# Values as the stationary operand in a decoder's first attention, with two transpose banks

## The chip, the core and the metric

The kernel runs on one core of a Trainium2 chip. A core has five engines that run their own instruction lists side by side and wait for each other through semaphores: TensorE (PE in the profile, with its weight loads as PEld), VectorE (DVE), ScalarE (ACT), GpSimd (POOL) and SyncE (SP), which here only issues DMA transfers. The metric is the device time of one execution in microseconds, the median of the runs.

## The reference

Two decoder layers over x, 16 sequences of 64 tokens with 128 features, all in fp32. Each layer has three parts with a layer norm ahead of each: a self-mixing part, a cross-attention over 64 context tokens of 96 features, and a mixture of 8 experts. The change touches only the first part of the first layer:

```python
qkv = jnp.einsum('bse,ef->bsf', inputs, qkv_kernel) + qkv_bias
qkv_heads = qkv.reshape(b, heads, s, -1)          # 16 heads, 64 rows, 3 x 8
q, k, v = jnp.split(qkv_heads, 3, axis=-1)
qk = jnp.einsum('bhse,bhte->bhst', q, k) * scale
attn = jax.nn.softmax(qk + causal_mask, axis=-1)
out = jnp.einsum('bhst,bhte->bhse', attn, v).reshape(b, s, e)
x = x + out
...
```

The reshape of (s, 384) to (heads, s, 24) cuts the token axis: one head of a sequence consists of 4 tokens, each of which gives 16 rows of 24 numbers. So a head has 64 rows and 8 features, and the head's output has to be put back into 4 tokens of 128 features.

## The kernel before, in words

The program is written by hand for each engine, in one list of calls per engine (`transpose_probs(3)`, `weigh_values(2)`, ...). The lists were ordered by a planner, and their order is the order of work on that engine; semaphores set only who waits for whom. PSUM has eight banks of 128 x 512 fp32 (`bank[0]` to `bank[7]`).

*Into the attention.* The projected q, k and v are stored to a scratch array in memory and loaded back with heads in place of features (SP, lines 389 and 394). A few spreading operations make block forms of them: KB and QA, and for the values Vb, a view of the tile `att`, which is filled with zeros first (line 449) and given a column of ones per head (line 487).

*The attention* works on 16 units u of eight heads each, two units being one pair m of sequences. On TensorE:
- `scores(m)` (lines 749 and 758) writes the causal mask and the scores of units 2m and 2m+1 to two of the banks 0 to 3.
- VectorE then does `row_max(u)` (line 1843) and `subtract_max(u)` (line 1850) into one of three buffers Es, and ScalarE `exponentials(u)` (line 1413) in place.
- `transpose_probs(u)` (line 776) transposes the four 128 x 128 blocks of Es to bank 4, and ScalarE's `copy_probs(u)` (line 1419) copies them to one of two buffers PTs. The next transposes wait for that copy.
- `weigh_values(u)` (line 792) has eight products. The transposed probabilities are the stationary operand (128 x 64); the values, 8 features and a one for two heads, are the moving operand (18 columns). Outputs go to bank 5 or 6, with 64 query rows on each half of the partitions; the ninth column is the sum of the probabilities.
- VectorE's `inverse(u)` and `normalise(u)` (lines 1829 and 1835) divide by these sums, into a tile with positions on the partitions.

An fp32 product is two records of matmul and two of weight load in the trace.

*Out of the attention*, per half of the batch h: `outputs_by_feature` (line 804) transposes, ScalarE copies (line 1427), SP stores to the scratch array `o_scratch` (line 418) and loads it back with features on the partitions (line 421), and `outputs_by_token` (line 822) transposes to tokens, which VectorE's `add_attention` (line 1856) adds to X. The layer norm of the cross-attention follows. Once all scores are out, SP also issues the weights of the last expert block (lines 425 and 427), whose place in Wb is then free.

*Behind it* stand the cross-attention (with the keys and values of the second layer, `keys_values1`, as filler), the first experts (`up0_first`, `up0_third`, `down0`, lines 884, 897 and 916), the state-space part of the second layer (`inject`, `widen`, lines 928 and 936; `add_states` on VectorE), the second cross-attention (`scores1`, `weigh_values1`, lines 976 and 999) and the last experts with a search for the routing threshold (`count`, line 1068).

## Time and profile before

| | |
|---|---|
| Runs | 257.46 us median (256.94 to 261.43, three runs) |
| Span of the profiled execution | 255.3 us (its own time beside this span was not recorded) |
| TensorE busy | 239.0 us, 94% |
| VectorE busy | 175.9 us, 69% |
| ScalarE busy | 141.8 us, 56% |
| GpSimd busy | 77.9 us, 31% |
| Granted TensorE clock | full speed in every stretch that was asked for |

The span runs from the first to the last instruction of one execution. A busy share is a mean over stages with different limits; which engine sets the time of a stage is read from the chain of waits, which follows the work back from the last instruction to what released it.

### The profile page before, as it was taken

How to read it: one execution, taken by the hardware profiler on the slowest of the kernel's cores; microseconds unless marked ns; L12 is line 12 of the kernel's file. 1: busy time of each engine (PE TensorE's matmuls, PEld its weight loads, DVE VectorE, ACT ScalarE, POOL GpSimd, SP SyncE). 2: the span in 40 equal slices, each digit the busy share in tenths (PEclk: the TensorE clock that was granted, in tenths of full speed). 3: DMA queues.
4: the chain of work that ended last, by engine and by line, in shares of the span. 5: the costliest groups of instructions: out<-in, count | busy, mean ns of one | idle time of the engine just before them, and what ended most of it. 6: DMA issues, size and time to landing. Idle time of an engine off the chain costs nothing.

```text
span 255.3 us, 5508 instructions
## 1 busy us (share of the span) xinstructions
PE 239.0 (94%) x1993; PEld 163.9 (64%) x1994; DVE 175.9 (69%) x602; ACT 141.8 (56%) x293; POOL 77.9 (31%) x137
## 2 busy tenths in 40 slices
PE   8988899998999999999999886999998999999995
PEld 8555577774535766756593534678887566577775
DVE  5465699874878836445217979957655688889975
ACT  0764776764264688467657445465565744544540
POOL 7856900001040474667465051533401000000000
DMA  5888960178100000000000000000000000000002
GB/s 136 173 196 245 302 152 0 31 220 205 44 1 0 1 3 0 0 1 3 0 1 3 1 0 0 3 3 3 3 5 0 3 0 0 1 3 0 0 3 82
DMA packets 24040, 11.64 MB, mean 46 GB/s; under 512 B 13017, under 2 KB 23006, under 8 KB 24014
## 3 DMA queue, kind: packets, MB, share of 16 engines
q1 hardware_dynamic: 22973, 10.94, 16.5%
q0 software_dynamic: 80, 0.20, 0.7%
q8 instruction: 16, 0.26, 0.4%
q10 hardware_dynamic: 960, 0.16, 0.3%
q14 instruction: 11, 0.08, 0.1%
HBM read 8.68 MB, written 2.62 MB: 44 GB/s over the span
## 4 chain that ended last, share of the span: by engine, by line
PE 73%; DVE 15%; ACT 5%; issue 3%; POOL 2%; DMA 1%; DVEq 0%; POOLq 0%; ACTq 0%
PE bank L1029 10%; PE bank L1041 10%; PE bank L897 6%; PE bank L884 6%; PE bank L916 6%; PE bank L776 3%; DVE stats L1720 3%; PE bank L1014 3%; PE bank L758 2%; PE bank L976 2%; PE bank L648 2%; PE bank L792 2%; PE bank L693 2%; PE bank L986 2%; PE bank L999 2%
## 5 line engine op out<-in xcount | busy, mean ns | idle before, releaser
L516 POOL TENSOR_TENSOR X<-X,att 128x128 f32<-128x128 f32 x72 | 30.4, 457 | 29.2 <-ACT att L1469 29.1
L441 POOL TENSOR_TENSOR rs<-rs,halves 128x4 f32<-128x4 f32 x14 | 14.9, 1063 | 61.8 <-DVE rs L1735 61.1
L1029 PE MATMUL bank<-XT,Wb 128*128 128x512 f32 x64 | 29.9, 599 | 0.0
L1041 PE MATMUL bank<-Wb,att 128*128 128x128 f32 x224 | 27.2, 278 | 0.0
L1041 PEld LDWEIGHTS bank<-Wb,att 128*128 128x128 f32 x224 | 26.1, 192 | 1.4 <-issue 1.4
L1905 DVE SCALAR_TENSOR_TENSOR att<-bank,cols,att 128x512 f32<-128x512 f32 x18 | 13.5, 749 | 16.8 <-ACT att L1458 7.8
L1469 ACT ACTIVATE att<-bank,comb 128x128 f32<-128x128 f32 x72 | 20.2, 383 | 6.9 <-PE bank L916 6.8
L1509 ACT ACTIVATE att<-bank 128x512 f32<-128x512 f32 x32 | 18.7, 599 | 9.7 <-PE bank L1029 9.7
L916 PEld LDWEIGHTS bank<-W2a,att 128*128 128x128 f32 x144 | 18.0, 192 | 5.0 <-issue 3.6
L916 PE MATMUL bank<-W2a,att 128*128 128x128 f32 x144 | 18.7, 276 | 0.0
L884 PE MATMUL bank<-XT,W1a 128*128 128x512 f32 x36 | 18.2, 595 | 0.0
L897 PE MATMUL bank<-XT,W3a 128*128 128x512 f32 x36 | 18.1, 598 | 0.0
L1517 ACT ACTIVATE big<-bank 128x512 f32<-128x512 f32 x14 | 8.3, 596 | 17.1 <-PE bank L1041 17.1
L1458 ACT ACTIVATE att<-bank,cols 128x512 f32<-128x512 f32 x18 | 12.6, 699 | 9.5 <-DVE att L1905 7.1
L1029 PEld LDWEIGHTS bank<-XT,Wb 128*128 128x128 f32 x64 | 11.2, 192 | 9.4 <-issue 8.8
L2042 DVE SCALAR_TENSOR_TENSOR X<-big,rt,X 128x128 f32<-128x128 f32 x56 | 15.4, 347 | 2.6 <-ACT big L1517 2.4
L1742 DVE TENSOR_SCALAR XN<-X,mv,rs 128x128 f32<-128x128 f32 x48 | 14.1, 356 | 4.1 <-POOL rs L441 3.8
L1720 DVE BATCH_NORM_STATS2 stats<-X 128x6 f32<-128x128 f32 x48 | 10.4, 280 | 7.1 <-POOL X L516 5.3
L1419 ACT ACTIVATE PTs<-bank 128x512 f32<-128x512 f32 x16 | 9.5, 595 | 8.0 <-PE bank L776 5.8
L529 POOL TENSOR_TENSOR Es<-Es,sm 128x512 f32<-128x512 f32 x8 | 8.2, 1044 | 14.2 <-DVE sm L1965 14.2
L1843 DVE TENSOR_REDUCE mx<-bank 128x8 f32<-128x512 f32 x16 | 10.5, 678 | 2.4 <-PE bank L758 2.4
L776 PE MATMUL bank<-ident,Es 128*128 128x128 f32 x64 | 10.2, 283 | 1.9 <-ACT PTs L1419 1.6
(229 smaller groups left out, 484.1 us busy)
## 6 DMA issues: line engine op xcount, KB each, us to landing
Wb<-in_L_ffn_W SPq DMA_DIRECT2D x1, 1024.0 KB, 5.5
Wb<-in_L_ffn_W SPq DMA_DIRECT2D x8, 128.0 KB, 5.2
X<-in_x SPq DMA_DIRECT2D x2, 256.0 KB, 3.1
k_scratch<-QKVT SPq DMA_DIRECT2D x1, 512.0 KB, 3.9
q_scratch<-QKVT SPq DMA_DIRECT2D x1, 512.0 KB, 4.7
Wb<-k_scratch SPq DMA_DIRECT2D x1, 512.0 KB, 4.6
v_scratch<-QKVT SPq DMA_DIRECT2D x1, 512.0 KB, 6.1
V<-q_scratch SPq DMA_DIRECT2D x1, 512.0 KB, 6.2
```

The lines of the kernel that those rows point to most:

```text
L441: nc.gpsimd.tensor_tensor(rs[:, 0, cut], rs[:, 1, cut], halves[:, :], ALU.pow).then_inc(l_root[h], 1)
L516: nc.gpsimd.tensor_tensor(X[:, h * HT + t, :], X[:, h * HT + t, :], part0[:, i % 2, t, :], ALU.add).then_inc(f_acc, 1)
L776: last = nc.tensor.transpose(bank[4][:, p4 * P:(p4 + 1) * P], Es[:, u % 3, p4 * P:(p4 + 1) * P], ident[:, :])
L884: mm(bank[i % 2][:, :], W1a[:, e, :], XT[:, half(h)], start=True, stop=True).then_inc(f_h1, 1)
L897: mm(bank[2 + i % 2][:, :], W3a[:, e, :], XT[:, half(h)], start=True, stop=True).then_inc(f_h3, 1)
L916: last = mm(bank[4 + i % 2][:, t * P:(t + 1) * P], hid0[:, i % 2, t * P:(t + 1) * P], W2a[:, e, :], start=not shared, stop=True, skip_grou ...
L1029: mm(bank[i % 4][:, :], W1b[:, e, f * P:(f + 1) * P], XT[:, half(h)], start=True, stop=True).then_inc(m_up, 1)
L1041: last = mm(bank[4 + h][:, t * P:(t + 1) * P], hid[:, e % 2, f, tile], W2b[:, e, f, :], start=(f == 0), stop=(f == F1 - 1))
L1469: AF(part0[:, i % 2, t, :], bank[4 + i % 2][:, t * P:(t + 1) * P], ACT.Copy, scale=comb[:, tt, e:e + 1]).then_inc(f_part, 1)
L1509: AF(hid[:, e % 2, f, half(h)], bank[i % 4][:, :], ACT.Gelu).then_inc(m_gelu, 1)
L1720: last = V.bn_stats(stats[:, t, :], src[:, t, :])
L2042: last = V.scalar_tensor_tensor(X[:, t, :], ys[:, e, t, :], rt[:, 9, t, e:e + 1], X[:, t, :], ALU.mult, ALU.add)
```

## The change

Five things are done in the first attention.

1. `weigh_values` works on pairs m. The values of one head are the stationary operand (128 x 32: two blocks of 16 columns, the first nine of which are used, the sum's column among them), and the transposed probabilities stream as 64 columns. Sixteen products per pair go in turn to the four groups of 32 output partitions of bank 6.
2. `transpose_probs` writes to banks 4 and 5 in turn, so it waits for the copy of the unit before the last.
3. The division leaves the units. ScalarE's `values_out(m)` copies the undivided outputs and sums from bank 6. `inverse`, `normalise` and `outputs_by_feature` go.
4. The scratch array has whole rows (128 x 1024 per half), stored in one transfer and loaded in four: two for the outputs, two for the sums, in pieces of 256 bytes.
5. The sums are transposed to tokens (`sums_by_token`), inverted (`sums_inverse`), and `add_attention` multiplies the token outputs by them before it adds.

The zero fill of `att` now covers the whole tile and stands later in GpSimd's list. All lists were written out anew, in the last expert block too, where a loop stood before.

```diff
-    VW = HD + 1
+    VW = 16
...
-        Opos = att[:, VP:VP + N].rearrange("p (h q e b u) -> p h q e b u", h=2, q=NP4, e=HD, b=HB)
-        OT2 = big[:, 12 * N:12 * N + HALF].rearrange("p (c x) -> p c x", c=CH)
+        OV = [big[:, first:first + N].rearrange("p (c y t m) -> p m y c t", c=CH, m=HT, t=GT) for first in (12 * N, 15 * N)]
+        OVrows = [big[:, first:first + N] for first in (12 * N, 15 * N)]
...
-                sp.wait_ge(o_act[h], 1)
-                sp.dma_start(o_d[h, :, :].rearrange("(c e) (b u x) -> e b u c x", e=HD, b=HB, u=2)
-                             .rearrange("e b u c x -> (e b u) c x"), OT2).then_inc(st_o[h], 16)
+                sp.wait_ge(a_out, HT * (h + 1))
+                sp.dma_start(o_d[h, :, :], OVrows[h]).then_inc(st_o[h], 16)
                 sp.wait_ge(st_o[h], 16)
-                sp.dma_start(OT[:, half(h)], o_d[h, :, :]).then_inc(ld_o[h], 16)
+                blocks = o_d[h, :, :].rearrange("(j n v) (c x) -> n v c j x", j=NP4, n=2, c=CH)
+                for n in range(2):
+                    sp.dma_start(OT[:, half(h)].rearrange("p (n j x) -> p n j x", n=2, j=NP4)[:, n, :, :],
+                                 blocks[n, 0:HD, :, :, :].rearrange("e c j x -> (e c) j x")).then_inc(ld_o[h], 16)
+                for n in range(2):
+                    sp.dma_start(SU[:, half(h)].rearrange("c (n j x) -> c n j x", n=2, j=NP4)[:, n, :, :],
+                                 blocks[n, HD, :, :, :]).then_inc(ld_s[h], 16)
...
-            nc.gpsimd.memset(att[:, 0:VP], 0.0).then_inc(c_fill, 1)
...
+            nc.gpsimd.memset(att[:, :], 0.0).then_inc(c_fill, 1)
+            pool.wait_ge(c_fill, 4)
...
             def transpose_probs(u):
                 pe.wait_ge(a_exp, u + 1)
-                if u >= 1:
-                    pe.wait_ge(a_trc, u)
-                else:
+                if u >= 2:
+                    pe.wait_ge(a_trc, u - 1)
+                if u == 0:
                     pe.wait_ge(v_copied, 1)
+                if u == 1:
+                    pe.wait_ge(pow_ready, 1 + len(POWER_OF))
                 for p4 in range(NP4):
-                    last = nc.tensor.transpose(bank[4][:, p4 * P:(p4 + 1) * P],
+                    last = nc.tensor.transpose(bank[4 + u % 2][:, p4 * P:(p4 + 1) * P],
                                                Es[:, u % 3, p4 * P:(p4 + 1) * P], ident[:, :])
...
+            def weigh_values(m):
+                pe.wait_ge(a_trc, 2 * m + 2)
+                if m == 0:
                     pe.wait_ge(vb_act, 2)
...
+                if m >= 1:
+                    pe.wait_ge(a_out, m)
+                for i in range(NP4):
+                    for j in range(NP4):
+                        head = NP4 * j + i
+                        u2, first = head // HD, (head % HD) * S
+                        last = mm(bank[6][j * 2 * VW:(j + 1) * 2 * VW, i * S:(i + 1) * S],
+                                  Vb[:, m, head, :, :].rearrange("p n v -> p (n v)"),
+                                  PTs[:, u2, first:first + S], start=True, stop=True)
...
+            def sums_by_token(h):
+                pe.wait_ge(ld_s[h], 32)
...
+                for t in range(HT):
+                    last = nc.tensor.transpose(bank[7 - 2 * h][:, t * CH:(t + 1) * CH],
+                                               SU[:, half(h)].rearrange("c (x m) -> c m x", m=HT)[:, t, :], ident[0:CH, 0:CH])
...
             def outputs_by_token(h):
-                pe.wait_ge(ld_o[h], 16)
+                pe.wait_ge(ld_o[h], 32)
                 if h == 0:
-                    pe.wait_ge(o_act[0], 1)
+                    pe.wait_ge(o_inv[0], 1)
...
             def copy_probs(n):
                 act.wait_ge(a_tr, n + 1)
                 if n >= 2:
-                    act.wait_ge(a_pv, n - 1)
-                AF(PTs[:, n % 2, :], bank[4][:, :], ACT.Copy).then_inc(a_trc, 1)
+                    act.wait_ge(a_pv, n // 2)
+                AF(PTs[:, n % 2, :], bank[4 + n % 2][:, :], ACT.Copy).then_inc(a_trc, 1)
...
+            def values_out(m):
+                act.wait_ge(a_pv, m + 1)
+                AF(OV[m // HT][:, m % HT, :, :, :], bank[6][:, 0:2 * P].rearrange("p (y c t) -> p y c t", c=CH, t=GT), ACT.Copy
+                   ).then_inc(a_out, 1)
...
+            def sums_inverse(h):
+                dve.wait_ge(o_sums[h], 1)
+                V.reciprocal(rO[:, h, :, :], bank[7 - 2 * h][:, 0:HT * CH].rearrange("p (t c) -> p t c", c=CH)
+                             ).then_inc(o_inv[h], 1)
...
             def add_attention(h):
                 dve.wait_ge(x_psum[h], 1)
-                then(V.tensor_tensor(X[:, tiles(h), :], bank[7 - h][:, :].rearrange("p (t d) -> p t d", d=D),
-                                     X[:, tiles(h), :], ALU.add))
+                dve.wait_ge(o_inv[h], 1)
+                then(V.tensor_tensor(XN[:, tiles(h), :].rearrange("p t (c e) -> p t c e", e=HD),
+                                     bank[7 - h][:, :].rearrange("p (t e c) -> p t c e", e=HD, c=CH),
+                                     rO[:, h, :, :].unsqueeze(3).broadcast_to([P, HT, CH, HD]), ALU.mult))
+                then(V.tensor_tensor(X[:, tiles(h), :], XN[:, tiles(h), :], X[:, tiles(h), :], ALU.add))
```

How the order moves, at three places. TensorE, the last units of the attention, before (L776 are transposes of probabilities, L792 the value products, L822 the first half's outputs by token, L767 filler, L804 the second half's outputs by feature):

```order
L792 MATMUL bank<-att,PTs 64x18 x8
L776 MATMUL bank<-ident,Es 128x128 x4
L792 MATMUL bank<-att,PTs 64x18 x8
L822 MATMUL bank<-ident,OT 128x128 x4
L776 MATMUL bank<-ident,Es 128x128 x4
L792 MATMUL bank<-att,PTs 64x18 x8
L776 MATMUL bank<-ident,Es 128x128 x4
L792 MATMUL bank<-att,PTs 64x18 x16
L767 MATMUL bank<-causal,perm 128x512 x2
L804 MATMUL bank<-ident,att 128x128 x4
```

The same place now (L784 transposes, L755 and L764 scores, L800 value products, L812 sums, L830 outputs by token, L675 filler):

```order
L784 MATMUL bank<-ident,Es 128x128 x8
L755 MATMUL bank<-causal,perm 128x512 x2
L764 MATMUL bank<-big,Wb 128x4x64 x4
L800 MATMUL bank<-PTs,att 32x64 x16
L784 MATMUL bank<-ident,Es 128x128 x8
L800 MATMUL bank<-PTs,att 32x64 x16
L812 MATMUL bank<-ident,big 128x16 x4
L830 MATMUL bank<-ident,OT 128x128 x4
L784 MATMUL bank<-ident,Es 128x128 x8
L800 MATMUL bank<-PTs,att 32x64 x16
L675 MATMUL bank<-maskf,Wk 128x512
```

Two units of transposes stand together, and one group of value products follows a pair; ahead of the last two groups no scores are left. After the last group comes other work at once, no transpose of outputs.

ScalarE in the same stretch, before (L1413 exponentials, L1419 copies of transposed probabilities, L1427 outputs by feature):

```order
L1413 ACTIVATE Es<-Es 128x512 x2
L1419 ACTIVATE PTs<-bank 128x512 x2
L1427 ACTIVATE big<-bank 128x4x16x4 x2
L1413 ACTIVATE Es<-Es 128x512 x2
L1419 ACTIVATE PTs<-bank 128x512
L1413 ACTIVATE Es<-Es 128x512
L1419 ACTIVATE PTs<-bank 128x512 x2
```

and now (L1452 exponentials, L1458 copies of transposed probabilities, L1462 `values_out`):

```order
L1452 ACTIVATE Es<-Es 128x512 x2
L1458 ACTIVATE PTs<-bank 128x512 x2
L1462 ACTIVATE big<-bank 128x4x16x4
L1452 ACTIVATE Es<-Es 128x512 x2
L1462 ACTIVATE big<-bank 128x4x16x4
L1458 ACTIVATE PTs<-bank 128x512 x2
```

Each pair has one more copy, which stands in line with the exponentials and the copies of the next pair.

TensorE at the end of the first experts, before (L916 and L912 are down-projections and their bias, L936 `widen`):

```order
L916 MATMUL bank<-W2a,att 128x128 x4
L936 MATMUL bank<-ST,Apow 128x2x60
L936 MATMUL bank<-ST,Apow 128x2x56
L936 MATMUL bank<-ST,Apow 128x2x52
L912 MATMUL bank<-b2a,OT 128x128 x4
L916 MATMUL bank<-W2a,att 128x128 x4
L936 MATMUL bank<-ST,Apow 128x2x48
```

and now (L924, L920 and L944):

```order
L924 MATMUL bank<-W2a,att 128x128 x4
L920 MATMUL bank<-b2a,OT 128x128 x4
L924 MATMUL bank<-W2a,att 128x128 x4
L944 MATMUL bank<-ST,Apow 128x2x60
L944 MATMUL bank<-ST,Apow 128x2x56
L944 MATMUL bank<-ST,Apow 128x2x52
L944 MATMUL bank<-ST,Apow 128x2x48
```

The group `widen(0, 1)` of three matmuls has moved from before the last down-projection to behind it.

## Rows read from the trace of the kernel before

**Rows 1.** The page, busy us with share of span and instruction count.

```profile
PE 239.0 (94%) x1993; PEld 163.9 (64%) x1994; DVE 175.9 (69%) x602; ACT 141.8 (56%) x293; POOL 77.9 (31%) x137
```

**Rows 2.** Busy time by stage: stretch, length, then PE, PEld, DVE, ACT, POOL, clock, DMA.

```profile
26.50:59.30 32.80, 30.23 (x414) 23.31 (x416) 27.85 (x75) 21.43 (x39) 6.14 (x5) 1.00 0.56 146
59.30:80.80 21.50, 20.52 (x113) 10.78 (x113) 14.72 (x56) 10.60 (x19) 2.59 (x2) 1.00 0.21 47
80.80:134.70 53.90, 53.90 (x295) 35.97 (x294) 26.45 (x77) 35.87 (x98) 31.45 (x72) 1.00 0.00 1
134.70:161.30 26.60, 21.54 (x164) 11.34 (x162) 23.54 (x90) 13.05 (x24) 8.59 (x10) 1.00 0.01 2
```

**Rows 3.** Chain of waits in the attention: start us, us, what.

```profile
35.27 0.61 ACT PTs L1419
...
36.02 0.63 PE bank L776 x4
36.64 0.32 PE bank L749 x2
36.97 0.86 PE bank L758 x8
...
48.42 1.04 PE bank L792 x32
...
58.61 0.66 PE bank L792 x16
```

**Rows 4.** Chain of waits in later stages.

```profile
94.18 0.86 PE bank L897 x2
...
126.76 0.36 PE bank L928 x8
...
129.06 0.66 PE bank L936 x6
...
165.13 0.62 PE bank L999 x32
```

**Rows 5.** VectorE by line, 26 to 62 us: form, count, busy us, mean ns, idle before.

```profile
L1850 DVE TENSOR_TENSOR Es<-bank,mx 128x512 f32<-128x512 f32 x16 | 10.6, 679 | 0.6 <-PE bank L776 0.4
L1843 DVE TENSOR_REDUCE mx<-bank 128x8 f32<-128x512 f32 x16 | 10.5, 678 | 2.4 <-PE bank L758 2.4
L1835 DVE TENSOR_TENSOR att<-bank,rO 128x64 f32<-128x64 f32 x16 | 3.7, 259 | 0.2
L1829 DVE RECIPROCAL rO<-bank 128x8 f32<-128x8 f32 x16 | 3.0, 194 | 2.5 <-PE bank L792 2.5
```

**Rows 6.** ScalarE by line, 20 to 62 us.

```profile
L1413 ACT ACTIVATE Es<-Es 128x512 f32<-128x512 f32 x16 | 9.6, 627 | 2.4 <-DVE Es L1850 2.2
L1419 ACT ACTIVATE PTs<-bank 128x512 f32<-128x512 f32 x16 | 9.5, 595 | 8.0 <-PE bank L776 5.8 <-PE bank L792 2.1
L1427 ACT ACTIVATE big<-bank 128x256 f32<-128x256 f32 x4 | 1.3, 383 | 2.3 <-PE bank L804 2.3
```

**Rows 7.** Timeline, SP's issues and the transposes behind them: start us, us, instruction.

```profile
53.06 5.13 SPq L427 DMA_DIRECT2D Wb<-in_L_ffn_W  x8
...
61.23 0.37 SPq L418 DMA_DIRECT2D o_scratch<-big  x1
...
64.19 0.34 SPq L421 DMA_DIRECT2D OT<-o_scratch  x1
...
66.94 0.53 PEld L822 LDWEIGHTS bank<-ident,OT 128*128 128x128 f32 x4 [0.51 <-DMA OT<-o_scratch]
```

**Rows 8.** Transfers: issues, KB each, median us from issue to landing.

```profile
v_scratch<-QKVT SPq DMA_DIRECT2D x1, 512.0 KB, 6.1
...
o_scratch<-big SPq DMA_DIRECT2D x2, 256.0 KB, 3.0
```

**Rows 9.** Timeline of GpSimd: the fill of att, and its wait for the keys.

```profile
1.65 2.02 POOL L449 MEMSET att<- 128x2304 f32 x1
...
21.04 6.81 POOL L494 TENSOR_SCALAR big<-Wb,pairs 128x512 f32<-128x512 f32 x4 [4.20 <-DMA Wb<-k_scratch]
```

More of the change, by code:

```diff
@@ L533, in _ @@
             root(2, 0)
+            root(2, 1)
             add_part(0, 0, 0)
@@ L808, in power @@
+                last.then_inc(o_sums[h], 1)
             def power(r):
@@ L1069, in count @@
                    start=True, stop=True).then_inc(r_cnt, 1)
-            def count_next(rounds):
-                i = next(rounds, None)
-                if i is not None:
-                    count(i)
-                if i == SEARCH:
-                    prefix()
             def prefix():
@@ L1308, in _ @@
             up1(0, 1, 1)
[L1310 to L1320 removed]
+            up1(1, 0, 0)
+            count(0)
+            up1(1, 1, 0)
+            up1(1, 0, 1)
+            count(1)
+            down1(0, 1)
+            count(2)
+            up1(1, 1, 1)
+            up1(2, 0, 0)
+            count(3)
+            up1(2, 1, 0)
+            up1(2, 0, 1)
+            count(4)
+            down1(1, 0)
+            count(5)
+            down1(1, 1)
+            count(6)
+            up1(2, 1, 1)
+            up1(3, 0, 0)
+            count(7)
+            up1(3, 1, 0)
+            up1(3, 0, 1)
+            count(8)
+            down1(2, 0)
+            count(9)
+            down1(2, 1)
+            count(10)
+            up1(3, 1, 1)
+            up1(4, 0, 0)
+            up1(4, 1, 0)
+            count(11)
+            up1(4, 0, 1)
+            up1(4, 1, 1)
+            up1(5, 0, 0)
+            count(12)
+            down1(3, 0)
+            count(13)
+            down1(3, 1)
+            count(14)
+            up1(5, 1, 0)
+            up1(5, 0, 1)
+            up1(5, 1, 1)
+            count(15)
+            prefix()
+            down1(4, 0)
+            down1(4, 1)
+            down1(5, 0)
+            down1(5, 1)
+            up1(6, 0, 0)
+            up1(6, 1, 0)
+            up1(6, 0, 1)
+            down1(6, 0)
+            up1(6, 1, 1)
+            up1(7, 0, 0)
+            up1(7, 1, 0)
+            up1(7, 0, 1)
+            up1(7, 1, 1)
+            down1(6, 1)
             down1_last()
@@ L2232, in _ @@
             route()
-            for e in range(E1 - 1):
-                add_expert(e)
+            add_expert(0)
+            add_expert(1)
+            add_expert(2)
+            add_expert(3)
+            add_expert(4)
+            add_expert(5)
+            add_expert(6)
             add_last()
```

471 lines of the change are left out of this document (211 added, 260 removed).

## Prediction

> **What bounds the kernel now.** I read five views. The page's busy shares come first [rows 1]: TensorE 94% of the span, everything else far below; that is an average. The busy time by stage is second [rows 2]; I cut the span where the work changes. The reader is to see that the first attention (26.5 to 59.3 us) has TensorE busy for 30.2 of 32.8 us and VectorE for 27.9; that the feed-forward behind it (80.8 to 134.7) has TensorE busy throughout; and that from 134.7 to 161.3 VectorE leads. So a gain in the attention survives if TensorE reaches the feed-forward earlier: what follows there is a fixed amount of TensorE work.
>
> The chain of waits inside the attention is third [rows 3]. It runs mostly on TensorE, but it also goes through ScalarE's copy of the transposed probabilities: copy, then the next transpose, since all transposes use bank 4. Two batches of weigh_values take 1.04 us together; the last begins at 58.61 and ends at 59.27 (its 0.66 added).
>
> The same chain in other stages shows what small matmuls cost [rows 4]; the lists by line give VectorE's and ScalarE's instructions [rows 5, 6]; the timeline of the transfers gives the way of the second half's outputs through memory [rows 7].
>
> **The change: value matmuls.** Before, 16 batches of 8 products (16 records each, since an fp32 product is two records): 32 records in 1.04 us [rows 3], so 8.3 us in all. Now there are 8 groups of 16 products, also 32 records each, with 64 moving columns, 32 output columns and four column groups in turn. No row has this shape with 64 columns. Bounds, per group: below, weigh_values1, 32 records of 64 moving columns over four quarters of the array, 0.62 us; above, the rate of inject, four groups of 32 columns but 128 moving columns, 8 records in 0.36 us, so 32 in 1.44; and with no overlap at all 16 times an eighth of a 512-column product, 16 x 0.86/8 = 1.72 [rows 4]. I take 0.62: inject has the same four groups, and its 0.36 for four 128-column products, which one after another would be 4 x 0.86/4 = 0.86, shows that the groups overlap; weigh_values1 has the same moving length. Saved on TensorE: 8 x (1.04 - 0.62) = 3.4 us. The feature transposes go (two groups of four, 0.63 us each by the transposes of [rows 3]); two groups of four 16-row transposes of the sums come. I cost these at 0.25 us each, estimated below a full group's 0.63.
>
> **VectorE** loses 16 reciprocals and 16 multiplies, 3.0 + 3.7 = 6.7 us [rows 5]. It gains two small reciprocals and two 128x512 multiplies, which I price as the subtraction of the same size, 0.68 each, and which lie in add_attention. **ScalarE** loses four 0.38 us copies and gains eight 128x256 copies out of the bank. Nearest row: those same copies, 0.383; with elements 16 bytes apart they could cost as much as a 512-element copy, 0.595, and not less than 0.383 [rows 6]. I take 0.383.
>
> **The period.** One period is two batches of scores (0.32 + 0.86), two groups of transposes (2 x 0.63) and a value group (0.62): TensorE 3.06 us [rows 3, 4]. ScalarE: 2 x 0.627 + 2 x 0.595 + 0.383 = 2.83 [rows 6], and five hand-overs of some 0.04, so 3.03. VectorE: 2 x (0.679 + 0.678) = 2.71 [rows 5]. Three engines within 0.35 us, in fixed orders: I take 3.2. Added waits: a value group waits until ScalarE has emptied the one before (0.383), with transposes and scores in between to cover it; the copies of a pair wait for the value group of the pair before, which is in the period. The second transpose bank is what lets TensorE write one group while ScalarE still copies the other. Start: the first transposes wait for scores 1.2, two maxima 1.36 (the second maximum now stands ahead of the first subtraction), a subtraction 0.68 and an exponential 0.63: 26.5 + 3.9 = 30.4. The eighth period starts at 30.4 + 7 x 3.2 = 52.8. Sums and outputs of the first half stand ahead of it: 0.25 + 0.63 and a wait of some 0.4 for the reciprocal. Then transposes 1.26, the uncovered copy 0.6 + 0.1, the group 0.62: it ends near 56.7, not 59.27. That is **-2.6**.
>
> **The way out of the second half.** Before, from the end of the last batch (59.27) to the store (61.23) stood reciprocal, multiply, transposes and copies: 1.96 us [rows 3, 7]. Now one copy: 56.7 + 0.4 = 57.1, 4.1 earlier. But the last block's weights go through the same queue. Their last eight issues took from 53.06 to 58.19, and the store came 3.0 us after; now they follow the last scores, 30.4 + 5 x 3.2 + 1.3 + 1.2 = 48.9, end near 54.6, and the store comes 2.5 us after. It took 3.0 us, and the slowest store of a scratch array in this kernel 6.1 [rows 8]; below 3.0 I see no reason to go, since it writes twice the bytes (in 128 long rows instead of 2048 pieces). I take 4.0, nearer to its own row. The reload is four issues of some 0.4 us instead of one: outputs land one issue later, the sums two more behind them. So the outputs are transposed near 57.1 + 4.0 + 0.4 + 2.8 = 64.3; before 66.94 [rows 7]. Lead: 2.6. VectorE then has a multiply and a reciprocal more before the layer norm, 0.68 + 0.20, so **1.7** of lead arrives, and TensorE, in order, enters the feed-forward 1.7 earlier.
>
> **Behind it.** The tables were written anew for all engines. In the feed-forward TensorE has the same work. One place changes the path: the group widen(0, 1), 0.66 us [rows 4], stood ahead of the last down-projection and now stands behind it, and that projection's output starts the VectorE-bound stage: **-0.7**. add_bias moves behind two weigh_probs on POOL, which is idle for two thirds of that stage [rows 2]: nothing. The fill of att grows from 2304 to 4096 columns and moves to just before the ones in it. At 2.02 us for 2304 it takes 3.6; POOL waited 4.2 us there for keys from memory [rows 9], which cover it by 0.6. Without that cover the late halves of the keys would slip, and only scores(4), the fifth of eight, needs them. The count rounds of the last block: the first stands one up-projection earlier (0.86), but the end follows TensorE's work: nothing. At the start v is projected ahead of the context; its store can leave up to one projection earlier (0.86), but q's load, on which the first scores wait, keeps its place in SP's order: nothing.
>
> **Sum:** -2.6 + 0.9 (lead lost on the way out) - 0.7 = -2.4. The profiled execution has a span of 255.3; the median of the three runs is 257.46, 2.2 above that span. So 252.9 of span, and **255.0** of time. A measurement of this kernel tells about 2% from no change (under 252.3, over 262.6).
>
> **A rule against the change.** In [rows 6] ScalarE's copies are already 0.6 of each 1.2 us that it spends on a batch, and now it alone empties the value bank. By those rows it is 0.03 us a period below TensorE. The Trainium skill (TensorEngine Tiling (Array Packing), section Performance Considerations) says that tiling speeds up TensorE but not the emptying of PSUM, that the copies may become the limit, and that both ScalarE and VectorE should share them; by that rule ScalarE sets the period here. What it makes of the time is the second rival.
>
> **Rivals.**
> - *The four column groups do not overlap* (or at inject's rate). The decision point is a value group of 0.76 us: above it TensorE's period passes 3.2. At 1.44 the stage grows by 8 x 0.68 = 5.4: 260.4, slower than before; at 1.72, 262.7. For it: no row with 64 columns in four groups, and inject's rate if it is per record. Against: inject's own 0.36 instead of 0.86. 5%.
> - *ScalarE sets the period, nothing is won.* If the strided copy costs 0.595 and every exponential waits its turn in ScalarE's order, the period is 3.5 to 3.7, as now (8 of them fill most of the 32.8 us). Then only widen and part of the way out are left: about 257. For it: three engines nearly equal, latencies uncovered at the last two periods. Against: VectorE had 6.7 us more and that goes. 17%.
> - *The reload lands late.* Store 6.1 instead of 4.0 because the last block's weights are ahead of it in the queue, reload the same with four times the issues: outputs near 68 or 69. TensorE has some 7.7 us of work between (59.27 to 66.94 before), to about 64.4, so it waits some 4 us: 259. For it: the shorter distance to the weights. Against: the same store took 3.0. 5%.
> - *More is won.* The whole lead of 4.1 is kept, the extra VectorE work hides behind the sums, and the search's earlier start gives its 0.86: -4.1 - 0.7 - 0.9 = 251.8. 18%.
>
> The forecast itself has 55%: 252.9 to 257. The range is 251.6 to 258.2: it leaves out part of the last rival and both slow ones. Faster by over 2%: most of "more is won", 0.17. Slower by over 2%: 0.04 (the groups without overlap, or two of these at once). Within: 0.79.
>
> **What would show it.** Value groups of 32 records at about 0.6 us in the chain; the line of the copies out of the transpose banks gone from the chain between transposes; the last value group ending near 56.7; the second half's outputs transposed near 64.3; the stage from 80.8 and the one from 134.7 moved earlier by 1.7 and 2.4 us with the same lengths. It is wrong if a value group takes over 0.76, if ScalarE has no idle time in the attention, or if TensorE waits for the reload.

## The result, and the profile after

The changed kernel takes 256.33 us (median of 20 runs, 254.86 to 261.34); the kernel before, run beside it, 257.42 (20 runs, 256.94 to 261.43). The ratio is 0.9941, with a 95% interval from 0.9918 to 0.9964: a small gain, within 2%. The forecast was 255.0, with a range of 251.6 to 258.2.

The times are told here together with the mean granted TensorE clock of each run, because without it they can't be understood: of the 20 runs of the change one had a mean clock of 0.999 and took 254.86 us; eight at 0.993 took 255.18 to 256.11; seven at 0.986 or 0.987 took 255.62 to 257.48; the four at 0.98 or less took 257.88 to 261.34.

The profiled execution took 256.76 us, span 255.0, mean clock 0.986. Its page, in the form of [rows 1], and the row of the granted clock in 40 slices of the span (a digit is tenths of full speed):

```profile
PE 238.0 (93%) x1994; PEld 162.3 (64%) x1994; DVE 173.3 (68%) x574; ACT 142.3 (56%) x297; POOL 79.3 (31%) x137
PEclk9999599999999999999999999999999999999999
```

VectorE has 2.6 us less work than in [rows 1], TensorE 1.0 less. New is the 5: in the fifth slice TensorE ran at about half its clock. The windows below are read as [rows 2]: stretch, length, busy us of PE, PEld, DVE, ACT, POOL, then the clock, the share of DMA, GB/s.

```profile
23.00:24.00 1.00, 0.42 (x4) 0.28 (x2) 0.00 (x0) 0.67 (x2) 0.91 (x2) 1.00 0.58 193
25.00:26.00 1.00, 0.38 (x3) 0.09 (x2) 0.45 (x1) 0.83 (x3) 0.91 (x2) 0.91 0.91 324
26.00:27.00 1.00, 0.59 (x3) 0.56 (x5) 0.13 (x1) 0.27 (x1) 0.91 (x2) 0.50 1.14 348
...
31.00:32.00 1.00, 1.00 (x6) 0.35 (x5) 0.19 (x1) 0.95 (x2) 0.93 (x2) 0.50 1.22 304
32.00:33.00 1.00, 1.00 (x8) 1.00 (x6) 1.00 (x2) 0.16 (x1) 0.37 (x1) 0.67 0.98 298
...
26.50:59.30 32.80, 30.19 (x420) 21.87 (x421) 25.36 (x49) 23.81 (x44) 6.57 (x6) 0.91 0.60 168
```

From just before 26 to about 32.7 us the clock is at 0.50, which is 1.2 GHz of 2.4. In the microseconds before, TensorE was busy for 0.42 and 0.38 of a microsecond: the new early order has the key products done earlier, and TensorE then waits for copies of the powers and for q. The kernel before has its key products there; the same view of it shows it at full clock:

```profile
23.00:24.00 1.00, 1.00 (x5) 0.37 (x5) 0.00 (x0) 0.83 (x2) 1.00 (x1) 1.00 0.70 277
...
25.00:26.00 1.00, 0.78 (x5) 0.29 (x3) 0.59 (x1) 0.51 (x2) 1.00 (x1) 1.00 0.98 283
```

The chain of waits of the changed kernel, through the attention and out of it (start us, us, what; compare [rows 3]):

```profile
26.41 2.08 PE bank L764 x8
28.49 1.04 PE bank L740 x4
...
30.07 1.71 PE bank L764 x8
31.78 1.46 PE bank L784 x8
...
33.56 0.86 PE bank L764 x8
...
37.66 0.58 PE bank L800 x32
...
49.49 0.65 PE bank L800 x32
...
56.21 0.70 PE bank L800 x32
...
56.93 0.61 ACT big L1462
...
57.56 4.19 DMA o_scratch<-big
...
62.18 2.69 DMA OT<-o_scratch
...
64.92 0.75 PE bank L830 x4
65.66 0.59 PE bank L812 x4
66.28 0.57 DVE rO L1900
...
66.94 0.70 DVE XN L1919
67.67 0.70 DVE X L1922
```

Eight score records (the second group, at 30.07) take 1.71 us at half clock and 0.86 at full; the four transposes of the values take 1.04, and 0.66 at full clock in the profile of c3 below. Value groups take 0.58 to 0.70. The last ends at 56.91 us; before it was 59.27 [rows 3]. The second half's outputs are transposed at 64.92; before 66.94 [rows 7]. Then come two steps in line that the kernel before didn't have there: the sums' transposes and the reciprocal, and a product (L1919) ahead of the sum (L1922).

ScalarE's and VectorE's lines, in the form of [rows 5, 6]:

```profile
L1462 ACT ACTIVATE big<-bank 128x256 f32<-128x256 f32 x8 | 4.9, 617 | 0.9 <-PE bank L800 0.8
...
L1900 DVE RECIPROCAL rO<-bank 128x64 f32<-128x64 f32 x2 | 1.1, 558 | 1.3 <-PE bank L812 1.3
```

How much of the lead is left further on has to be read where the same work is done in both orders. The first up-projection is no such mark: `up0_first` came first before (77.81), and now `up0_third` stands ahead of it and of the gate (75.35). Two marks that are: the transposes of the cross-attention behind one group of `up0_first` and two of `up0_third`, and the last down-projection of the first experts. Before:

```profile
80.46 0.38 PE L844 MATMUL bank<-ident,QKVT 128*128 128x128 f32 x2
132.29 1.16 PE L916 MATMUL bank<-W2a,att 128*128 128x128 f32 x8
```

and now:

```profile
79.77 0.38 PE L852 MATMUL bank<-ident,QKVT 128*128 128x128 f32 x2
132.20 1.16 PE L924 MATMUL bank<-W2a,att 128*128 128x128 f32 x8
```

The last product ends at 252.34 us (before 252.61). So in these two profiles 2.4 us are won at the end of the attention, 0.7 are left where the feed-forward has begun, 0.1 at its last down-projection, and 0.3 at the end.

### The profile page after: what moved, and what is told of

Read it like the earlier page. It is cut to its first block, busy times and chain, and to the rows that moved or that the text cites. A ratio compares the mean times of both kernels' runs of the same rounds, so it can differ in the third digit from the quotient of the medians.

```text
span 255.0 us, 5486 instructions
## 1 busy us (share of the span) xinstructions
PE 238.0 (93%) x1994; PEld 162.3 (64%) x1994; DVE 173.3 (68%) x574; ACT 142.3 (56%) x297; POOL 79.3 (31%) x137
## 4 chain that ended last, share of the span: by engine, by line
PE 70%; DVE 15%; DMA 7%; ACT 3%; issue 2%; POOL 1%; SPq 0%; DVEq 0%
PE bank L1037 11%; PE bank L1049 10%; PE bank L924 7%; PE bank L905 6%; PE bank L892 5%; PE bank L1022 3%; PE bank L764 3%; PE bank L784 3%; DMA V<-q_scratch 3%; PE bank L640 3%; PE bank L984 2%; DVE stats L1795 2%; PE bank L800 2%; PE bank L654 2%; DMA q_scratch<-QKVT 2%
## 5 line engine op out<-in xcount | busy, mean ns | idle before, releaser
L446 POOL TENSOR_TENSOR rs<-rs,halves 128x4 f32<-128x4 f32 x14 | 14.3, 1022 | 81.3 <-DVE rs L1810 77.8
L924 PEld LDWEIGHTS bank<-W2a,att 128*128 128x128 f32 x144 | 18.3, 191 | 6.2 <-issue 4.0
L924 PE MATMUL bank<-W2a,att 128*128 128x128 f32 x144 | 19.1, 278 | 0.0
L1369 ACT ACTIVATE XT<-bank 128x512 f32<-128x512 f32 x12 | 7.1, 593 | 9.0 <-PE bank L654 9.0
L1458 ACT ACTIVATE PTs<-bank 128x512 f32<-128x512 f32 x16 | 8.8, 595 | 4.4 <-PE bank L784 4.4
```

Of the source, the lines that this page charges most:

```text
L446: nc.gpsimd.tensor_tensor(rs[:, 0, cut], rs[:, 1, cut], halves[:, :], ALU.pow).then_inc(l_root[h], 1)
L924: last = mm(bank[4 + i % 2][:, t * P:(t + 1) * P], hid0[:, i % 2, t * P:(t + 1) * P], W2a[:, e, :], start=not shared, stop=True, skip_grou ...
```

## Experiments

Line numbers move with the edits. **Where the clock went** was the first question. My theory: TensorE falls to 1.2 GHz because it idles at 23 to 26 us, and that costs what the change wins. The rivals: q's load sets the start anyway, or what is won early is lost later.

**a1_hold**: the gaps filled.

```diff
+            def hold(n):
+                for _ in range(n):
+                    mm(bank[4][:, 0:P], XT[:, 0:P], XT[:, 0:P], start=True, stop=True)
...
                 if m == 0:
+                    hold(4)
                     pe.wait_ge(kb_early, NP4)
...
+            hold(3)
             power(5)
+            hold(2)
             power(6)
```

> The changed kernel with nine plain fp32 products of 128 columns added on TensorE (three ahead of the fifth group of powers, two ahead of the sixth, four in the first scores group between its mask products and its wait for keys and queries); their results go to a bank that nobody reads. They fill the gaps of 22.95 to 26.4 us. Theory A, the clock: in the profile of the change TensorE idled there and its granted clock was 0.50 from about 26 to 32.7 us; the first eight score products took 2.08 us where the same eight took 0.86 before. With the gaps filled the granted clock is 1.00 in that stretch, the first score group takes 0.86, the first transposes start near 30.4 instead of 31.7, the last value group ends near 55.4 instead of 56.9, and the median goes from 256.3 to 254.9 (1.2 to 1.6 us less). Theory B, the start of attention is set by the load of q and by VectorE and ScalarE: the clock may come back, but the last value group ends within 0.4 of 56.9 and the median within 0.4 of 256.3. Theory C, what is won early is lost again behind the attention: the last value group ends near 55.4 and the median stays within 0.4 of 256.3.

Measured: 256.21 us median of 12, 254.66 to 260.18; ratio to the kernel before 0.9936 (0.9899 to 0.9973). Its windows:

```profile
24.00:26.00 2.00, 2.00 (x15) 1.54 (x15) 0.51 (x1) 1.71 (x4) 1.91 (x2) 1.00 0.88 305
...
156.00:158.00 2.00, 0.72 (x15) 0.50 (x17) 1.97 (x6) 0.63 (x1) 0.99 (x1) 1.00 0.00 0
...
160.00:162.00 2.00, 2.00 (x33) 1.78 (x32) 1.90 (x6) 0.72 (x2) 1.52 (x2) 0.50 0.00 0
```

The early clock is back, and the last value group starts at 54.45 us instead of 56.21, 1.8 us earlier, as theory A had it (1.5). But the median didn't follow, so its forecast of the time failed. The rows show why: in this execution the clock fell at 159 us instead, behind another stretch in which TensorE was busy for 0.72 of 2 us. (The change's own profile has 0.73 of 2 us there and keeps its clock, so such a stretch doesn't always bring a fall.) Five of the 12 runs stayed at 0.999 or 1.0, and these took 254.66 to 255.05; five at 0.987 took 256.78 to 257.92.

**a2_old_early** and **a3_new_early** exchange the early order alone, the lists of TensorE and ScalarE up to the first probabilities: a2 is the change with the list of before, a3 the reverse. The core of a2:

```diff
-            power(1)
-            keys0(0)
-            power(2)
...
+            power(4)
+            keys0(0)
+            power(5)
+            keys0(1)
+            power(6)
```

> The changed kernel with the order of the early work (first products to the first score groups, on TensorE and on ScalarE) as the kernel before has it; attention and everything behind it as changed. Theory A, the clock: TensorE again has its key products and powers at 23 to 25.3 us, the granted clock stays 1.00 from 25 to 33 us, and the median is 254.9 (1.2 to 1.6 us under the change). Theory B, the early order costs nothing, or gains: median within 0.4 of 256.3, or up to 1 us slower because the keys of the later cross attention are copied later.

Measured: 257.79 us median of 12 (257.20 to 261.12), no run above 0.993. Theory A failed here, and the median lies 0.5 above what theory B allowed.

```profile
30.00:32.00 2.00, 0.76 (x6) 0.66 (x7) 1.80 (x4) 1.75 (x4) 1.93 (x2) 1.00 1.22 298
32.00:34.00 2.00, 2.00 (x12) 1.50 (x12) 0.69 (x1) 2.00 (x4) 0.11 (x1) 0.58 0.98 281
```

With the old early order the clock holds to 32 us and falls then, behind a stretch in which TensorE was busy for 0.76 of 2 us while it waited for the first probabilities. So the early order alone isn't the cause: with the other order the gap lies elsewhere, and the fall came behind it.

> The kernel before with only the early order of the change, on TensorE and on ScalarE. Theory A, the clock: the granted clock falls to 0.50 at 26 to 32 us here too, the first score groups and transposes take twice as long, and the median is 1.0 to 1.8 us above the kernel before (258.4 to 259.2). Theory B, the early order is harmless: within 0.4 of 257.4.

Measured: 258.55 us median of 12 (256.79 to 261.71), ratio 1.0022 (0.9985 to 1.0059). Three runs at 1.0 took 256.79 to 257.34, as the kernel before does at 1.0 (256.94 to 257.55). So at full clock the early order itself costs nothing. Whether it makes more runs lose the clock isn't shown: 9 of 12 did, against 17 of 29 of the kernel before beside them (49 of 79 in all comparisons). The median lies where theory A had it, but the interval takes in no change as well as a loss of 1.5 us. The profiled execution has the same gap as the change, and kept its clock:

```profile
25.00:26.00 1.00, 0.36 (x3) 0.06 (x2) 0.46 (x1) 0.82 (x3) 0.91 (x2) 1.00 0.99 324
26.00:27.00 1.00, 0.60 (x6) 0.63 (x8) 0.11 (x1) 0.26 (x1) 0.91 (x2) 1.00 1.09 344
```

**b4_hold_both** also fills TensorE's gaps in the second cross attention.

```diff
+                    if t == 0:
+                        hold1(3)
                     pe.wait_ge(c_qc[t // HT], 4)
...
+            hold1(6)
             scores1(2)
             transpose_xn(4, 1, 6)
             scores1(3)
+            hold1(2)
             queries1(1, 0)
```

> The changed kernel with the nine filling products of the first experiment, and eleven more of 128 columns in the gaps of TensorE at 152 to 161 us (three before the second cross attention's first scores wait for their queries, six before its third score group, two behind its fourth). Their results are read by nobody. In the runs of the change the time follows the granted clock: 254.86 us at a mean of 0.999, 255.2 to 256.1 at 0.993, 256.5 to 257.5 at 0.987; with the first filling alone the five runs at 0.999 or 1.0 took 254.66 to 255.05 and the six at 0.992 to 0.987 255.6 to 257.9, and the profile of one of these had its 0.50 at 159 to 166 us. Theory A, the clock falls where TensorE idles: with both gaps filled nearly all runs are at 0.999 or more, and the median is 254.7 (1.6 under the change). Theory B, the falls at 159 us come whatever TensorE does: the runs split as with the first filling, and the median is 256.0 to 256.3.

Measured: 255.91 us median of 12 (255.13 to 259.21), ratio 0.9909 (0.9877 to 0.9942). Six of 12 runs at 0.999 or 1.0, where theory A had nearly all. In the profiled execution the clock fell at a third place, near 52 us, where TensorE waits ahead of the last value groups. The products themselves cost: the runs at 0.999 or 1.0 take 255.13 to 255.75, with the first nine products alone (a1) 254.66 to 255.05.

**c3_hold_lite** keeps seven of those eleven (three and four).

> The changed kernel with the nine early filling products and seven later ones (three and four; the four others of the kernel with both fillings are left out, since behind the read-out of the second half that kernel's profile took 104.57 us to the last product and the change's 104.08). Theory A: the runs stay at a mean clock of 0.999 or more as with all eleven, and the half microsecond comes back: median 254.8. Theory B: with fewer products the clock falls again in half of the runs: median 255.5 to 256.

Measured: 255.23 us median of 6 (254.68 to 255.73), ratio 0.9917 (0.9901 to 0.9933); five of the six at 1.0. In these runs the clock mostly stays, and the half microsecond came back in part (255.09 by the middle run at 1.0, b4 255.34).

**d1_before_hold** puts such products into the kernel before.

```diff
                 if m == 0:
+                    hold(4)
                     pe.wait_ge(kb_early, NP4)
...
+                    if t == 0:
+                        hold1(3)
                     pe.wait_ge(c_qc[t // HT], 4)
...
+            hold1(4)
             scores1(2)
```

> The kernel before, its own order and its own attention, with eleven filling products of 128 columns on TensorE (four ahead of the first scores' wait for keys and queries, three and four in the second cross attention's gaps at 152 to 160 us). Theory A, the granted clock falls where TensorE has idled: runs of the kernel before at a mean of 1.0 took 257.0 to 257.5 (18 of 51), and the filled one shows 1.0 in most runs and a median of 257.1. Then the change at an undisturbed clock is worth 257.1 against 254.7 to 255.3, 1.8 to 2.4 us, twice what its plain median shows. Theory B, the falls in the kernel before come from elsewhere: the runs split as before, median 257.5 to 258.4.

Measured: 257.47 us median of 12 (257.37 to 259.72), ratio 1.0006 (0.9976 to 1.0036). Nine of 12 runs at 1.0, where 30 of 79 runs of the kernel before are at 0.999 or more, but 8 of the 17 beside it. That points to TensorE's idling in this kernel too; 12 runs don't show it. It isn't faster, since the products cost the kernel before 0.3 to 0.4 us at full clock.

In all, the seven kernels with both gaps filled (b4, c3, b8, b7, b2h, c1, e1) had 40 of 52 runs at 0.999 or more; the change 1 of 20. The change was not run again beside them, so this compares different series of runs; the kernel before, which stood beside the seven, had 18 of 50.

**What the parts are worth.** **a4_one_bank** takes the second transpose bank away.

```diff
-                if u >= 2:
-                    pe.wait_ge(a_trc, u - 1)
+                if u >= 1:
+                    pe.wait_ge(a_trc, u)
...
-                    last = nc.tensor.transpose(bank[4 + u % 2][:, p4 * P:(p4 + 1) * P],
+                    last = nc.tensor.transpose(bank[4][:, p4 * P:(p4 + 1) * P],
```

> The changed kernel with one bank for the transposed weights instead of two: each transpose waits for the copy of the one before. If the period of the attention is set by TensorE's work (3.06 us of it in 3.2), the wait for each copy, 0.6 us of ScalarE for every four transposes, puts about 0.5 us into each of eight periods that other matmuls cover in part: the last value group ends 1 to 3 us later and the median is 1 to 3 us above the change. If other work always stands between two transposes, as in the kernel before, nothing: within 0.4 of 256.3.

Measured: 264.48 us median of 6 (261.52 to 266.46), ratio 1.0171 (1.0122 to 1.022). Its two runs at 1.0 took 261.52 and 261.76 us, 6.8 over the change at 0.999. The timeline of TensorE:

```profile
41.29 0.65 PE L800 MATMUL bank<-PTs,att 128*32 128x64 f32 x32
45.22 0.66 PE L800 MATMUL bank<-PTs,att 128*32 128x64 f32 x32
```

The period is 3.9 us instead of 3.0: in every one of the eight periods TensorE stands for 0.7 to 0.8 us between the two groups of transposes, waiting for the copy. (The clock of this execution fell only at 58 us.) The size was over twice what I expected; with one bank, in this order of work, the change would be slower than the kernel before.

**b8_no_division** (base: b4, both fillings) leaves out the division of the second half.

```diff
             outputs_by_token(1)
-            sums_by_token(1)
...
-            sums_inverse(1)
...
+                if h == 1:
+                    cut = X[:, tiles(h), :].rearrange("p t (c e) -> p t c e", e=HD)
+                    then(V.tensor_tensor(cut, bank[7 - h][:, :].rearrange("p (t e c) -> p t c e", e=HD, c=CH), cut, ALU.add))
+                    return
```

> The kernel with both fillings, and without the division of the second half's outputs: its sums are loaded but not transposed nor inverted, and the transposed outputs are added to the residual as they are, in one VectorE step. This leaves a part of the computation out. Theory A, the three steps in line (0.59, 0.57 and 0.70 in the profile of the change) are what ate the lead: 1.9 us less than with both fillings alone, or 1.4 to 1.9. Prediction's price for them was 0.25, 0.20 and 0.68, of which 0.88 on the path: 0.9 to 1.1 less. Theory B, something behind them sets the entry to the feed-forward stage: less than 0.3.

Measured: 254.11 us median of 6 (253.86 to 254.99), ratio 0.9848 (0.9797 to 0.99). At 0.999 or 1.0 it takes 253.86 to 254.13, both fillings alone 255.13 to 255.75: 1.2 to 1.4 less (254.09 against 255.34 by the middle runs at 1.0, 254.03 against 255.46 with those at 0.999). In the two profiles the way from the second half's transposes to the first `up0_first` takes 11.8 us, with the division 13.1: what is saved there arrives at the end. That lies between theory A and the prediction's price.

**b7_sums_hold** (same base) has the sums ahead of the outputs; on SP's queue too, the two loads into SU stand ahead of the two into OT.

```diff
+            sums_by_token(1)
             outputs_by_token(1)
-            sums_by_token(1)
```

> The kernel with both fillings, and the sums' loads ahead of the outputs' loads on SP's queue, and for the second half the sums' transposes ahead of the outputs' on TensorE (as the first half has them). In the profile of the change the second half's transposes at 64.92 are followed by the sums' transposes (0.59), the reciprocal (0.57), the product (0.70) and the sum (0.70); before, the sum alone followed. Theory A, these steps in line are what ate the lead of 2.0 us between 64.9 and 77: with the sums ahead, transposes and reciprocal lie beside the load of the outputs (2.69), which comes up to 0.9 later because it is queued second: the product begins 0.3 to 1.1 earlier and the median is 0.3 to 1.1 under that with both fillings alone. Theory B, the lead is lost to the order on TensorE ahead of the gate (transposes, queries and an up-projection in line from 73.6 to 77.1): no change, within 0.25.

Measured: 255.35 us median of 6 (255.23 to 257.06), as both fillings alone at full clock (255.34): no gain, as theory B had it. The timeline:

```profile
63.06 0.65 PE L817 MATMUL bank<-ident,big 16*128 16x16 f32 x4
63.64 0.75 PE L835 MATMUL bank<-ident,OT 128*128 128x128 f32 x4
...
64.02 0.42 DVE L1951 TENSOR_TENSOR QKVT<-QKVT,sm 128x256 f32<-128x256 f32 x1
64.36 0.55 DVE L1915 RECIPROCAL rO<-bank 128x64 f32<-128x64 f32 x1
65.02 0.69 DVE L1934 TENSOR_TENSOR XN<-bank,rO 128x512 f32<-128x512 f32 x1
```

The sums were there at 63.7, but the reciprocal waited in VectorE's list behind the cross attention's probabilities until 64.36, and the outputs came later, behind them. The product starts at 65.02; in c3's chain, with the sums behind, at 65.18.

**b2h_widen_back** (same base) puts widen(0, 1) back.

```diff
             down0(1, 7)
+            widen(0, 1)
             down0(1, 8)
-            widen(0, 1)
```

> The kernel with both fillings, and one widening step of the states (three products of 128 by 128 with 0.66 us a group, ahead of the read-out) put back ahead of the last down-projection, where the kernel before has it. The prediction took 0.7 us for its move behind that projection. Theory A, the move is worth that: 0.5 to 0.8 us slower than both fillings alone. Theory B, the step only waits for another engine's copy of the states at either place: within 0.25. Theory C, the move was a loss, since the read-out of the first half came 0.8 later in the change: 0.4 to 0.8 faster.

Measured: 255.50 us median of 11 (255.37 to 256.61), ten at 1.0; both fillings alone 255.34 at 1.0, b7 255.32. From the gate to the last product it took 176.0 us, b7 175.8. The move is worth about 0.2, not 0.7: theory B. The profiles show why: with the step behind the projection, the next step (`widen(0, 2)`) waits 0.38 us for VectorE's copy of the states, which the projection covers where the step stands ahead of it.

**c1_gate_early** (base: c3) moves the gate, on TensorE first, then on VectorE.

```diff
             cross0_q(1)
-            up0_third(0, 0)
-            cross0_scores(1)
             gate(0)
+            cross0_scores(1)
+            up0_third(0, 0)
...
+            gate0(0, 0)
             gate_first(0)
+            gate0(0, 1)
             gate_second(0)
-            gate0(0, 0)
```

> That kernel (nine and seven filling products) with the first half's gate moved ahead of the last cross-attention scores and of the first up-projection on TensorE, its softmax ahead of those scores' on VectorE and ScalarE, and the first two products of the feed-forward on VectorE ahead of the choice of experts; the gate's transposes go behind the second down-projection. Theory A, the gate's chain on VectorE (78.2 to 83.1 in the profile of the change) sets when the feed-forward gets going: 1.0 to 1.6 us less than without the move. Theory B, TensorE has work of its own from 66 us on (its gaps between 75 and 84 sum to under 0.5 us in the profile with the sums first): 0 to 0.4 less.

Measured: 254.93 us median of 5 (254.55 to 255.78), ratio 0.9906 (0.9889 to 0.9924): 0.3 under c3 (0.2 by the middle runs at 1.0), theory B. In its profile the clock fell near 52 us again:

```profile
51.00:52.00 1.00, 0.35 (x3) 0.25 (x3) 0.56 (x1) 0.59 (x2) 0.00 (x0) 1.00 1.07 340
52.00:53.00 1.00, 0.91 (x5) 0.94 (x6) 0.00 (x0) 0.00 (x0) 0.00 (x0) 0.57 1.08 369
```

The profile of c3 has the same 0.35 in that microsecond, and 1.00 of clock in the next.

**e1_way_out** (base: c1) shortens the way out: the nine loads of expert weights leave the loop over the halves and follow it, the first half's sums go to bank 1 instead of 7, and its outputs' transposes move up.

```diff
                 sp.dma_start(o_d[h, :, :], OVrows[h]).then_inc(st_o[h], 16)
...
-                if h == 0:
-                    sp.wait_ge(a_scores, NU)
...
+            sp.wait_ge(a_scores, NU)
...
+            outputs_by_token(0)
             weigh_values(6)
             sums_by_token(0)
-            outputs_by_token(0)
             transpose_probs(14)
```

> The kernel with the gate moved ahead, and four changes on the way out of the attention: the loads of the second layer's expert weights (nine, 5.7 us of issues on SP's queue, until 55.0 us) go behind both halves' stores and reloads; the first half's sums go to another bank, so that its outputs' transposes don't wait for the reciprocal (0.74 us in which TensorE stood, with the last probabilities' transposes queued behind); those outputs' transposes go into the wait ahead of the seventh value group; and the last probabilities' transposes follow the sums at once. Theory A, the end of the attention is set by what stands ahead of its last transposes on TensorE and the store then by SP's queue and by the transfers beside it: the last value group, at 54.4 us in the kernel with both fillings, starts near 53.1, the second half's outputs are transposed at 61.0 to 61.5 instead of 63.2, and the median is 1.0 to 1.7 us under that with the gate moved (253.2 to 253.9). Theory B, VectorE's list from 61 to 72 us or the first half's own chain sets the entry to the feed-forward: outputs earlier, but the median within 0.4 of 254.9.

Measured: 254.21 us median of 6 (253.98 to 254.84), ratio 0.9871 (0.9844 to 0.9898), all six at 1.0: the best version here, 0.7 under c1, between the theories.

```profile
53.38 0.65 PE L806 MATMUL bank<-PTs,att 128*32 128x64 f32 x32 [0.74 <-ACT PTs L1472]
...
61.41 1.03 PE L779 MATMUL bank<-causal,perm 128*128 128x512 bf16 x4 [0.16 <-issue]
62.27 0.63 PE L835 MATMUL bank<-ident,OT 128*128 128x128 f32 x4
...
54.73 0.34 SPq L418 DMA_DIRECT2D o_scratch<-big  x1
57.38 0.93 SPq L422 DMA_DIRECT2D OT<-o_scratch  x2
```

The store takes 2.65 us, from its issue to that of the loads, instead of 4.38 (c3's chain) now that the weights aren't beside it, and the loads leave at 57.4. But TensorE's list holds the outputs' transposes behind the first half's scores and filling products of its own (L779), until 62.27: the limit has become the order of the lists.

## Why the prediction was right, and where not

The time lies in the stated range, the gain is within 2% as forecast, and 255.0 is what the change takes at an undisturbed clock (254.86 in its one run at 0.999, 254.66 to 255.05 in a1's five). The median is 1.3 us above it. The chain of c3, whose profile is at 1.0, gives the steps without the clock's part, and its timeline the two marks of the feed-forward:

```profile
41.89 0.65 PE bank L805 x32
...
44.75 0.58 PE bank L805 x32
...
54.42 0.70 PE bank L805 x32
...
55.77 4.38 DMA o_scratch<-big
...
63.16 0.75 PE bank L835 x4
```

```profile
78.02 0.38 PE L857 MATMUL bank<-ident,QKVT 128*128 128x128 f32 x2
130.44 1.16 PE L929 MATMUL bank<-W2a,att 128*128 128x128 f32 x8
```

| against the kernel before, us | predicted | change's profile | c3, clock 1.0 |
|---|---|---|---|
| last value group ends (59.27) | -2.6 | -2.36 | -4.15 |
| second half's outputs transposed (66.94) | -2.6 | -2.02 | -3.78 |
| cross-attention's transposes in the feed-forward (80.46) | -1.7 | -0.69 | -2.44 |
| last down-projection starts (132.29) | -2.4 | -0.09 | -1.85 |
| last product ends (252.61) | -2.4 | -0.27 | -1.98 |

- *Value groups*: right. 0.58 to 0.70 us for 32 records, against 0.62; the four column groups overlap, so the first rival is out.
- *Period*: 2.96 us (37.66 to 49.49, four of them) instead of 3.2, though terms on both engines were off. The copy out of the value bank takes 0.617, not 0.383. I had both ends and took the wrong one: this copy writes its elements far apart and costs as much as a 512-element copy, 0.595 (no run has this copy with its elements side by side, so the cause is inferred). By these means ScalarE would need 2 x 0.631 + 2 x 0.595 + 0.617 = 3.07 a period, but its instructions overlap: two copies stand in c3's timeline at 1.09 together, two exponentials at 1.16, so 2.87. I had added five hand-overs instead. TensorE needs 2.86 (41.89 to 44.75 in c3, a period without a wait) and not 3.06, since two groups of transposes take 1.02 together. ScalarE is thus level with TensorE. The Trainium skill (TensorEngine Tiling (Array Packing), Performance Considerations) says that the copies may become the limit; the trace agrees in part, since ScalarE's copies stay in the chain of c3 ahead of the value groups at 38.80 and 47.70 and of the last two. But the period still fell, and the second rival is out.
- *Start*: "at the start ... nothing" is the step that failed. Transposes began at 31.8 instead of 30.4, since the clock was at 0.50. I had looked at what the new early order makes wait for data, and not at how long TensorE then stands. At full clock they began at 30.2 (a1, c3), as predicted. The Trainium skill (TensorE: Matmul & The Clock Gate, HAM oscillation — how this bites in real kernels) says that a wait between stretches of matmuls can put the engine back to the lower clock, so that the next stretch starts slow; the runs agree at five places, though TensorE was partly busy there and the fall came in some executions only.
- *Store and reload*: 4.19 predicted as 4.0, and the transposes at 64.92 as 64.3: right, and the third rival (68 or 69) is out; TensorE waited 0.16 us for the reload. The second half's store took 3.9 to 4.4 us where the weights' loads run beside it (the change, a1, b7, b8, c3), and 2.65 where they don't (e1); the first half's store, which has nothing beside it, took 2.6 to 3.5 in the same kernels and the others. So the weights cost it about 1 us.
- *Lead lost on the way out*: predicted 0.9, and 1.3 in both columns, from the second row to the third. The sums' transposes take 0.59 (0.25 predicted) and the reciprocal 0.57 (0.20); b8 puts the division at 1.2 to 1.4.
- *Behind it*: "in the feed-forward TensorE has the same work" is true, but the new order of that work takes longer, a term that I had at nothing. Between the two marks of the feed-forward stand 51.83 us before and 52.43 now (52.42 in c3), though a widening group of 0.75 has left the stretch: 1.3 us more. By the rows, 0.4 of it lies around the transposes of the experts' choice (there is a wait of 0.18 for VectorE behind the first), 0.4 in two groups of transposes of the normed tokens, which now follow down-projections (0.66 each instead of 0.44), and 0.3 in the down-projections. No run puts this order back, so which of its moves does it stays open.
- *Widen*: -0.7 predicted, 0.2 measured (b2h). I had counted the step's own duration, as if nothing waited for its result behind it.
- *More is won*: its first condition came true at full clock (4.15 us at the end of the attention); the division and the feed-forward's order took it back.
- *From span to time*: the sum added 2.2 us, a median over runs of mixed clocks less a span at full clock. In every profiled run that has both on record the difference is 1.7 to 1.8 (256.76 and 255.0 for the change), so the same sum should have read 254.7.

So the sum came out near because the shorter period (1.6 more, at full clock) paid for the store, the way out, the feed-forward's order and widen. That these cancel is luck. The clock then took about half of the gain: 2.2 us at full clock (254.86 against 257.1), 1.1 by the medians.

## What to carry to other kernels

Before a re-ordering is priced, look at the busy share of TensorE in the microseconds ahead of each dense stretch: work that is moved out of a gap can cost the clock of what follows, and filling products whose results nobody reads are a cheap test of that. Compare runs at the same mean granted clock before a difference of 1% is put down to an instruction. Where two orders are compared, read the lead at marks behind which the same work is left. And price a strided copy out of a bank, or a reciprocal over 64 columns, from the nearest row of the same access, not from the number of elements.

## What the runs showed that I had not expected

The granted clock fell to 0.50 at five places, each behind a stretch in which TensorE was partly idle: 26 us (change), 32 (a2), 52 (b4, c1), 58 (a4), 159 (a1). Such a stretch was also followed by no fall: at 26 us in a3, at 52 in c3, at 159 in the change. At half clock eight score records take 1.71 us instead of 0.86. The mean clock of a run came in steps (1.0, 0.993, 0.987, 0.98), and in the kernel before the time follows them: 256.9 to 257.6 at 1.0, 257.3 to 258.7 at 0.993, 259.7 to 260.2 at 0.987. Why the same program falls in some runs and not in others stays open: no run here separates it. A 512 KB store took 3.9 to 4.4 us beside the loads of the weights and 2.6 to 3.5 with nothing beside it.
